# Recurrent scan, layer norm and quantized FFN on one core: four rows to a partition, and a scan that adds place to place in PSUM

## The reference

```python
kv = ctx * ctx                      # k and v are both ctx
r_t = 0.9 * r_(t-1) + kv_t          # over the sequence, from zero
x = x + layernorm(x) * r            # one row of x has one mean and one spread
x = x + ffn(layernorm(x))           # 512 -> 2048 -> 512, weights w1, w2
```

## Time and profile before

| | |
|---|---|
| median of 3 runs | 1265.83 us (1264.18 to 1266.1) |
| the profiled execution | 1265.31 us |
| its span, first to last instruction | 1263.5 us |
| TensorE busy | 1213.5 us, 96% |
| ScalarE busy | 979.9 us, 78% |
| VectorE busy | 872.2 us, 69% |
| GpSimd busy | 162.3 us, 13% |
| mean granted TensorE clock | 0.987 of 2.4 GHz |

### The profile page before, as it was taken

How to read it: one execution, slowest core, us unless ns; L and a number is a source line. 1 busy time by engine, 2 the same in 40 slices (tenths; PEclk the granted TensorE clock), 3 DMA queues, 4 the chain that set the end, 5 groups by cost and what they waited for, 6 DMA issues and landing times.

```text
span 1263.5 us, 15533 instructions
## 1 busy us (share of the span) xinstructions
PE 1213.5 (96%) x5386; PEld 562.1 (44%) x5386; DVE 872.2 (69%) x1262; ACT 979.9 (78%) x1211; POOL 162.3 (13%) x394
## 2 busy tenths in 40 slices
PE   5998999999699999999999999799999999999997
PEld 2444444444344444444444444344444444444443
DVE  4887999886577777777777777566545655654554
ACT  4788999887577777777777776688887888888776
POOL 2646556444000000000000000000000000000000
PEclk9999999999799999999999999899999999999999
DMA  9999999972277799999999998699999999999998
GB/s 354 403 406 333 389 363 341 346 277 81 118 321 289 305 394 407 359 365 362 362 358 351 348 363 317 229 334 419 418 417 417 417 418 417 417 418 416 416 417 325
DMA packets 134614, 448.78 MB, mean 355 GB/s; under 512 B 10740, under 2 KB 10760, under 8 KB 123400
## 3 DMA queue, kind: packets, MB, share of 16 engines
q1 hardware_dynamic: 94744, 331.40, 66.2%
q10 hardware_dynamic: 39792, 116.40, 25.8%
HBM read 254.81 MB, written 192.94 MB: 354 GB/s over the span
## 4 chain that ended last, share of the span: by engine, by line
PE 80%; POOL 6%; issue 5%; DVE 4%; DMA 3%; ACT 2%; SPq 1%; ACTq 0%; POOLq 0%; DVEq 0%
PE ps L833 35%; PE ps L875 33%; PE ps L811 9%; PE ps L855 2%; DMA xq<-hidden_scratch 2%; POOL xq L444 2%; DVE st L644 1%; DVE st L630 1%; DVE xq L639 1%; DMA xq<-in_x_dram 1%; POOL rstd L436 1%; POOL cs_bc L428 1%; ACT xq L478 1%; ACT xq L589 0%; SPq L317 0%
## 5 line engine op out<-in xcount | busy, mean ns | idle before, releaser
L875 PE MATMUL ps<-w2T,xq 128*128 128x512 f16 x2048 | 446.4, 381 | 4.2 <-ACT xq L589 3.8
L833 PE MATMUL ps<-xq,w1T 128*128 128x512 f16 x2048 | 448.7, 380 | 1.4 <-DVE xq L710 1.4
L589 ACT ACTIVATE xq<-xq,hb,hs 128x512 f16<-128x512 f32 x494 | 357.3, 801 | 83.6 <-PE ps L875 57.5
L701 DVE TENSOR_REDUCE work<-xq 128x2 f32<-128x1024 f32 x255 | 311.0, 1220 | 125.9 <-ACT xq L534 125.9
L534 ACT ACTIVATE xq<-ps 128x1024 f32<-128x1024 f32 x255 | 260.9, 1023 | 123.1 <-PE ps L833 122.9
L875 PEld LDWEIGHTS ps<-w2T,xq 128*128 128x128 f16 x2048 | 200.0, 98 | 250.6 <-ACT xq L589 9.8
L811 PE MATMUL ps<-xq,work 128*128 128x512 f32 x640 | 283.0, 603 | 24.7 <-ACT xq L468 24.7
L833 PEld LDWEIGHTS ps<-xq,w1T 128*128 128x128 f16 x2048 | 199.1, 98 | 237.0 <-issue 1.9
L749 DVE TENSOR_TENSOR work<-ps,cs_bc 128x512 f32<-128x512 f32 x128 | 88.4, 691 | 185.0 <-PE ps L875 178.6
L811 PEld LDWEIGHTS ps<-xq,work 128*128 128x128 f32 x640 | 122.9, 193 | 178.0 <-issue 161.0
L478 ACT ACTIVATE xq<-ps,ones,cs_bc 128x512 f32<-128x512 f32 x128 | 98.9, 772 | 24.8 <-PE ps L811 23.8
(11 more groups left out here) (99 smaller groups left out, 444.9 us busy)
## 6 DMA issues: line engine op xcount, KB each, us to landing
hidden_scratch<-xq SPq DMA_DIRECT2D x240, 512.0 KB, 6.0
xq<-hidden_scratch SPq DMA_DIRECT2D x232, 512.0 KB, 21.2
work<-x_scratch ACTq DMA_DIRECT2D x42, 1024.0 KB, 11.4
xq<-in_ctx_dram ACTq DMA_DIRECT2D x31, 1024.0 KB, 9.2
xq<-in_x_dram SPq DMA_DIRECT2D x24, 1024.0 KB, 12.0
x_scratch<-xq SPq DMA_DIRECT2D x24, 1024.0 KB, 8.4
out_dram<-work ACTq DMA_DIRECT2D x24, 1024.0 KB, 12.0
xq<-in_L_ffn_w_dram SPq DMA_DIRECT2D x8, 1024.0 KB, 7.8
```

Of the source, the lines that this page charges most:

```text
L589: act.activation(hq[c % HQ], src[:, c % 2, :], ACT.Relu, bias=hb[:, q:q + 1], scale=hs[:, q:q + 1]).then_inc(h_scaled, 1)
L701: dve.tensor_reduce(hmax[:, b * NF + 2 * q:b * NF + 2 * q + 2], src, AX.X, ALU.max).then_inc(kept_maxed, 1)
L833: last = pe.matmul(bank, w1T[:, k, f * P:(f + 1) * P], xq_rows(b, k), start=(k == 0), stop=(k == KD - 1))
L875: last = pe.matmul(acc_bank(s, i), src[:, i * P:(i + 1) * P], w2T[:, q, :], start=first, stop=final)
```

## The change

Row `4 * p + i` of the sequence now stands in place i, partition p: a partition takes four consecutive rows, and a load or store of a batch has runs of 8 KB in memory instead of 2 KB. The scan of place 0 is the sum of four matmuls, one for each place. Place i then is place i - 1 times 0.9 plus its own rows. The factor 0.9 is put into the row's statistics (`half_x`, `per_row_x`, `eps_x`), so that the bank only needs one more matmul with a diagonal matrix (`own_mat`), added on to what is in the same bank, after place i - 1 has been read from it. A batch has one bank, seven matmuls. Batches are interleaved: the orders of tiles and of scans are the lists `tiles` and `scans`. There is a fourth slot for ctx (`CS`), x is loaded seven batches ahead (`LEAD`), the scaled scan has four slots of one tile instead of eight, and x statistics are made four batches ahead.

```diff
-CS = 3
+CS = 4
-LEAD = 5
+LEAD = 7
+    scans, tiles = [(0, 0), (0, 1)], [(0, 0), (0, 1)]
+    for j in range(NB):
+        ahead = j + 1 < NB
+        scans += ([(j + 1, 0)] if ahead else []) + [(j, 2), (j, 3)] + ([(j + 1, 1)] if ahead else [])
+        tiles += [(j, 2)] + ([(j + 1, 0)] if ahead else []) + [(j, 3)] + ([(j + 1, 1)] if ahead else [])
...
-    x_rows = x.rearrange("b (i p) d -> b p i d", p=P)
+    x_rows = x.rearrange("b (p i) d -> b p i d", p=P)
...
ScalarE:
-            load_ctx(1)
-            load_ctx(2)
+            for j in range(1, CS):
+                load_ctx(j)
             square(0)
+            factors(0, 0)
+            square(1)
+            factors(0, 1)
             for j in range(NB):
-                factors(j, 0)
-                factors(j, 1)
-                if j + 1 < NB:
-                    square(j + 1)
-                factors(j, 2)
+                factors(j, 2)
+                if j + 1 < NB:
+                    factors(j + 1, 0)
                 factors(j, 3)
+                if j + 1 < NB:
+                    factors(j + 1, 1)
                 if j + CS < NB:
                     load_ctx(j + CS)
+                if j + 2 < NB:
+                    square(j + 2)
                 for m in weights_at(j - 1):
                     int_weights(m)
...
VectorE:
+            for n in range(2, NU):
+                j, i = divmod(n - 2, NI)
+                product(n)
+                y_stats(n - 1)
+                x_stats(j + RING, i)
+                if i == NI - 1:
+                    for m in weights_at(j):
+                        weight_scales(m)
...
TensorE:
+            def scan_first(j):
+                pe.wait_ge(ctx_squared, j + 1)
+                if j >= 6:
+                    pe.wait_ge(scan_scaled, tile_at[(j - 6, NI - 1)] + 1)
+                for k in range(NI):
+                    last = pe.matmul(scan_bank(j), decay_mat[:, k * P:(k + 1) * P], ct[j % CS][:, k, :], start=(k == 0), stop=(k == NI - 1))
                 last.then_inc(scan_ready, 1)
+            def scan_next(j, i):
+                pe.wait_ge(scan_scaled, tile_at[(j, i - 1)] + 1)
+                pe.matmul(scan_bank(j), own_mat[:, (i - 1) * P:i * P], ct[j % CS][:, i, :], start=False, stop=True, skip_group_check=True).then_inc(scan_ready, 1)
             pe.wait_ge(dve_step, 1)
+            scan_first(0)
+            pe.wait_ge(dve_step, NI)
+            scan_next(0, 1)
             for j in range(NB):
-                pe.wait_ge(ctx_squared, j + 1)
-                for i in range(NI):
-                    scan(j, i)
+                if j + 1 < NB:
+                    scan_first(j + 1)
+                scan_next(j, 2)
+                scan_next(j, 3)
+                if j + 1 < NB:
+                    scan_next(j + 1, 1)
                 for m in weights_at(j - 2):
                     turn_weights(m)
```

More of the change, by code:

```diff
@@ L86, in build @@
     quarters = [(w, k) for w in range(2) for k in range(4)]
+    scans, tiles = [(0, 0), (0, 1)], [(0, 0), (0, 1)]
[3 more added lines that the diff above has]
+        tiles += [(j, 2)] + ([(j + 1, 0)] if ahead else []) + [(j, 3)] + ([(j + 1, 1)] if ahead else [])
+    scan_at = {t: n for n, t in enumerate(scans)}
+    tile_at = {t: n for n, t in enumerate(tiles)}
     def weights_at(j):
@@ L187, in build @@
         hq = [xq[:, n * S:(n + 1) * S] for n in range(HQ)]
-        g1 = [arena[:, n * ROW:(n + 1) * ROW].rearrange("p (i d) -> p i d", i=NI) for n in range(2)]
-        ct = [arena[:, (2 + n) * ROW:(3 + n) * ROW].rearrange("p (i d) -> p i d", i=NI) for n in range(CS)]
+        g1 = [arena[:, n * D:(n + 1) * D] for n in range(NI)]
+        ct = [arena[:, (1 + n) * ROW:(2 + n) * ROW].rearrange("p (i d) -> p i d", i=NI) for n in range(CS)]
         w_stage = [arena[:, (5 + n) * ROW:(6 + n) * ROW] for n in range(2)]
         w_ints = [arena[:, 7 * ROW + n * (ROW // 2):7 * ROW + (n + 1) * (ROW // 2)].bitcast(F16) for n in range(2)]
-        carried = [work[:, 3 * ROW + ROW // 2 + n * 2 * D:3 * ROW + ROW // 2 + (n + 1) * 2 * D].rearrange("p (i d) -> p i d", i=2)
-                   for n in range(2)]
         decay_mat = work[:, 2 * ROW:2 * ROW + 4 * P]
+        own_mat = work[:, 2 * ROW + 4 * P:2 * ROW + 7 * P]
         diag_cs, diag_bq = ot[:, 0, :], ot[:, 1, :]
@@ L387, in _ @@
             gp.memset(ones[:, :], 1.0)
-            gp.memset(decays, DECAY)
+            gp.memset(decays, DECAY ** NI)
+            for i in range(NI):
+                gp.memset(half_x.rearrange("p (n i) -> p n i", i=NI)[:, :, i], 0.5 * DECAY ** -i)
+                gp.memset(per_row_x.rearrange("p (n i) -> p n i", i=NI)[:, :, i], DECAY ** (-2 * i) / D)
+                gp.memset(eps_x.rearrange("p (n i) -> p n i", i=NI)[:, :, i], LN_EPS * DECAY ** (-2 * i))
             gp.memset(neg_half[:, :], -0.5)
@@ L393, in _ @@
             gp.wait_ge(gp_step, 1)
-            for m, w in ((impulse, 4 * P), (ident[:, :], P), (ident_b[:, :], P)):
+            for i in range(NI):
+                part = impulse[:, i * P:(i + 1) * P]
+                gp.affine_select(out=part, in_=part, compare_op=ALU.not_equal, fill=DECAY ** (NI - i) if i else 1.0, base=1 if i else 0,
+                                 pattern=[[-1, P]], channel_multiplier=1)
+            for i in range(1, NI):
+                gp.memset(decays[:, i * P:i * P + 1], 0.0)
+            for m in (ident[:, :], ident_b[:, :]):
                 last = gp.affine_select(out=m, in_=m, compare_op=ALU.not_equal, fill=1.0, base=0,
-                                        pattern=[[-1, w]], channel_multiplier=1)
+                                        pattern=[[-1, P]], channel_multiplier=1)
             last.then_inc(consts_ready, 1)
@@ L415, in row_stats @@
                 gp.tensor_tensor(mean, t[0], factor[:, 0:n], ALU.mult)
-                gp.tensor_tensor(t[3], t[1], per_row[:, 0:n], ALU.mult)
-                step(gp.tensor_tensor(t[4], t[2], half[:, 0:n], ALU.mult))
-                gp.tensor_tensor(t[5], t[3], eps[:, 0:n], ALU.add)
+                gp.tensor_tensor(t[3], t[1], per[:, 0:n], ALU.mult)
+                step(gp.tensor_tensor(t[4], t[2], halves[:, 0:n], ALU.mult))
+                gp.tensor_tensor(t[5], t[3], floor[:, 0:n], ALU.add)
                 step(gp.tensor_tensor(t[6], t[4], t[4], ALU.mult))
@@ L433, in y_stats @@
                 gp.wait_ge(stats2_in, js[-1] + 1)
-                var = row_stats(pw2, stats_of(st2, js), mean2[:, columns(js)], half)
+                var = row_stats(pw2, stats_of(st2, js), mean2[:, columns(js)], half, per_row, half, eps)
                 gp.tensor_tensor(zrow[:, columns(js)], stats_of(rowmax, js), mean2[:, columns(js)], ALU.subtract)
@@ L475, in factors @@
                 act.activation(xi, xi, ACT.Identity, bias=nmean1[:, u:u + 1])
-                act.wait_ge(scan_ready, u + 1)
-                wait_count(act, x2_done, u + 1 - 2 * NI)
-                act.activation(g1[j % 2][:, i, :], scan_bank(j, i), ACT.Identity, bias=ones[:, 0:1],
+                act.wait_ge(scan_ready, scan_at[(j, i)] + 1)
+                wait_count(act, x2_done, n + 1 - len(g1))
+                act.activation(g1[n % len(g1)], scan_bank(j), ACT.Identity, bias=ones[:, 0:1],
                                scale=rstd1[:, u:u + 1]).then_inc(scan_scaled, 1)
@@ L611, in _ @@
             link(dve.tensor_tensor_scan(decay_mat, decays, impulse, 0.0, ALU.mult, ALU.add))
+            for i in range(1, NI):
+                link(dve.tensor_scalar(own_mat[:, (i - 1) * P:i * P], ident[:, :], DECAY ** -i, None, ALU.mult))
             def weight_scales(m):
@@ L632, in x_stats, with product, y_stats @@
                     ins.then_inc(stats1_in, 1)
-            def product(j, i):
+            def product(n):
+                j, i = tiles[n]
                 if i == 0 and j >= RING:
                     dve.wait_ge(stats2_ready, y_group[j - RING] + 1)
-                dve.wait_ge(scan_scaled, j * NI + i + 1)
+                dve.wait_ge(scan_scaled, n + 1)
                 xi = xt[j % XS][:, i, :]
-                dve.tensor_tensor_reduce(xi, g1[j % 2][:, i, :], xi, 1.0, -3.0e38, ALU.mult, ALU.max,
+                dve.tensor_tensor_reduce(xi, g1[n % len(g1)], xi, 1.0, -3.0e38, ALU.mult, ALU.max,
                                          rowmax[:, j % RING * NI + i:j % RING * NI + i + 1]).then_inc(x2_done, 1)
-            def y_stats(j, i):
-                dve.wait_ge(x2_done, j * NI + i + 1)
+            def y_stats(n):
+                j, i = tiles[n]
+                dve.wait_ge(x2_done, n + 1)
                 ins = dve.bn_stats(st2[:, j % RING * NI + i, :], xt[j % XS][:, i, :])
@@ L646, in y_stats @@
                     ins.then_inc(stats2_in, 1)
-            for j in range(3):
+            for j in range(RING):
                 for i in range(NI):
                     x_stats(j, i)
[L651 to L660, removed]
+                if j == 1:
+                    product(0)
+                    product(1)
```

(6 more changed lines are left out.)

28 lines of the change are left out of this document (13 added, 15 removed).

## The result

The changed kernel takes 1409.47 us (median of 4 runs, 1404.91 to 1410.16) against 1265.59 before. The ratio (of the means) is 1.1131, with a 95% interval from 1.1106 to 1.1156. I had said 1406, range 1363 to 1440. The profiled execution took 1410.16 us, with a span of 1408.4 and a mean granted clock of 0.931.

What follows compares the result with a forecast made beforehand. TensorE was taken as the bound, only partly in the scan stage. Last scaling moves from 315.09 to 416.2 (+101.1, span 1364.6); clock falls add 39 (1403.7), and 2.3 more gives 1406 us, range 1363 to 1440.

Steps and rivals of the forecast that it cites:

- The stages that the change doesn't touch: Second and third stages, two matmul groups of 2048: TensorE nearly always busy, so they give and lose nearly nothing.
- The ring: Scan stage: square, four matmuls and scalings wait on each other in turn; 10.9 us a turn against 8.6.
- The weight turns: Turns 2 to 17, preparing weights: ScalarE waits for GpSimd's statistics; a pair takes 29.2 or 27.9 us, not 21.9.
- The bias that waits for the statistics: ScalarE's second tile in odd weight turns: wanted at 11.6 us, comes at 18.95 (w1) or 17.6 (w2).
- the odd turn's fall: Weight turns: a clock fall costs 1.7 us; only the eight even turns' falls were taken to cost nothing.
- The clock: Scan stage: TensorE's granted clock falls in each turn's wait, 1.7 us each; 23 counted, 39 us.
- the clock stays up: Rival, scan stage: the clock doesn't fall in the short waits; 1367 us, chance 12%.
- the queue in GpSimd doesn't show: Rival, weight turns: statistics come early enough, so their wait doesn't show; 1366 us, chance 5%.
- the square could come early enough: Rival, scan stage: square ready some 4 us sooner, TensorE never stands; 18 us less, 1248, chance 5%.

Runs made afterwards that it cites:

- experiment 3: Changed kernel with ScalarE's square of batch j+2 after the second tile of a turn instead of the fourth: 1330.02 us (one run).
- experiment 4: Changed kernel with the square after the second tile and GpSimd's x statistics before the weight rounding: 1274.64 us, ratio 1.0075 to the kernel before.
- experiment 5: Kernel before the change with the square of the next ctx after the fourth tile instead of the second: 1356.34 us (one run).
- experiment 6: Kernel of experiment 4 with the square after the first tile of a turn instead of the second: 1342.68 us, ratio 1.0608 to the kernel before.
- experiment 7: Kernel of experiment 4 with the square ahead of the first tile of a turn: 1262.85 us, ratio 0.9987 to the kernel before.
- experiment 2: Kernel of experiment 1 with two or three unneeded fp32 matmuls added a turn and five scan banks instead of six: 1322.85 us (one run).
- experiment 1: Changed kernel with GpSimd making x statistics for the next pair of batches before it rounds weights: 1351.64 us (one run).

## Why the prediction was right, step by step

**The stages that the change doesn't touch**: right but for 3.4 us. From the last scaling of the first stage to the end it is 1408.4 - 456.56 = 951.8, against 1263.5 - 315.09 = 948.4. I had this at 0.

**The ring**: right. Turn at full clock 11.06, forecast 10.93; most of the difference is in the four matmuls (3.54 from the first's start to the next place's, not 3.44). Experiments 3, 4 and 5 show that the place of the square sets it, in both scans. I had called it a ring with nothing beside it. Experiments 6 and 7 show a second one beside it, through the matmul of (j+1,1), of 7.56 us, which is hidden in the changed kernel.

**The weight turns**: right in sum, and that in part by luck. With the clock, a pair was forecast at 29.2 + 1.7 for w1; 97.94 to 128.75 is 30.8. From turn 2 to turn 18 (55.96 to 298.86) it took 242.9 us, forecast 228.4 + 8 x 1.7 = 242.0. Two terms of it were wrong and cancel. The bias that waits for the statistics starts 17.48 us after the even turn does (86.88 to 104.36), not 18.95: VectorE's reduction starts at 8.02 as forecast, but from there the chain over GpSimd to the bias takes 9.46 us, not the 10.95 that I took from the kernel before, where the rounding alone took 4.10 us and here 3.12:

```profile
94.90 2.27 DVE L647 TENSOR_REDUCE wmax<-xq 128x4 f32<-128x2048 f32 x1
97.69 3.12 POOL L464 TENSOR_SCALAR xq<-xq,isw 128x512 f32<-128x512 f32 x4 [13.91 <-DVE isw L650]
```

Against that the odd turn's fall cost some 3 us (104.36 to 117.69 is 13.33, forecast 10.27), not 1.7, since the clock stayed low for 13.6 us there, four times as long as in a turn after the weights. Over the eight pairs the statistics came 9.2 us sooner than forecast, and the rest of the odd turns took 10.2 us more. In six of the eight pairs the even turn had no fall to hide (11.06); in the other two (13.77 and 12.76) the fall was hidden in front of the wait, as forecast.

**The clock**: right in its mechanism, and shown by experiment 2. The number of falls was wrong: 21 in the stage, not 31, as a third of the turns kept the clock; after the weight stretch they did so in spite of waits of 2.3 to 3.2 us just before the four. The falls were longer instead: the clock was low for 167 us of the stage. Take the 12 turns from 298.86 to 448.73: 149.9 us, 1.4 a turn above 11.06, where I had 1.7. By the rule of the Trainium skill ("TensorE: Matmul & The Clock Gate", "HAM oscillation — how this bites in real kernels"), which it tells of a loop with waits of about 3 to 5 us for transfers, every group after a wait starts slow. The trace agrees for two turns in three. My sum for the stage was 39 us for the clock, and 456.56 measured less 416.2 leaves 40. That the two agree so well is in good part chance: 4 of these 40 are the longer four matmuls, the falls in the odd weight turns were longer than I had them, the statistics' 9.2 us went the other way, and the first turn began 2 us late, with the clock low. Why the clock falls in some turns and not in others, with the same work in each, was not found.

**The rivals.** That the clock stays up (1367 us) did not come about. That the queue in GpSimd doesn't show I had priced at 1366; made so by experiment 1, it was 1351.64: the wait also brought slow clock, and without it the clock fell in every second turn, where I had it fall in each. That the square could come early enough I had priced at 1248; the nearest to it, experiment 7, gives 1262.85. I had said that it would decide if the square came some 4 us sooner. That was too simple: 2.5 us sooner gave 8.5 a turn, and 3.8 us sooner gave 9.36 at full clock (experiment 6), as ScalarE's other tiles are on TensorE's path too. Experiment 7 did take the square out of the ring, and then the second ring held 7.56, not VectorE 7.2.

## What to carry to other kernels

Fewer matmuls were worth nothing here, where two engines hand work to each other in a ring: 82 us of TensorE's work went, and the stage became 141 us longer. Write down both engines' lists and follow one turn, with every instruction that stands ahead in either queue; the sum of the longest such ring is the turn, and a shorter one may lie just below it. Then try the instruction that closes it (here one square, the last in its turn) in each place, counting what it pushes back: at full clock a turn went from 11.06 to 8.51 to 9.36 to 7.56 us. And look at what a long wait does to the clock of the engine that it leaves idle.

## What the runs showed that I had not expected

- More work made it quicker: 88 more fp32 matmuls that nobody needs took 28.8 us off (experiments 1 and 2), since the granted clock fell from 2.4 to 1.2 GHz once in the stage instead of 18 times.
- The clock's falls settle into patterns: turns of 11.06 and 12.76 in alternation for 95 us, and then 13.65 four times in a row, with the same scan work in each turn. In experiment 1 the alternation lasts 190 us.
- The square one place earlier made the kernel 68 us slower (experiment 6): outside the weight stretch 0.85 us of each turn is a longer ring, and some 2 us more are the clock.
- Runs of 8 KB in memory in place of 2 KB for the stores of the result made a store land in 7.9 us instead of 11.8 and the kernel 0.2% slower (1.0011 to 1.0029).
